# Layer 3 attention probabilities turned in 32x32 blocks on VectorE and moved through DRAM, with new orders for layers 2 and 3

## The reference

```
# layer 2 (RWKV block): token shift, five mixes, k, r, v, g, decay w; state scan; group norm; gate; Wo;
#                       layer norm; channel mix with Wfk, Wfr, Wfv
# layer 3
q = hidden_state @ Wq + bq          # 32 query heads of 16
k = encoder_hidden_state @ Wk + bk  # 8 key heads
v = encoder_hidden_state @ Wv + bv
scores = einsum('bkgld,bksd->bkgls', q, k) * scale + mask
attn = softmax(scores, axis=-1)                    # 32 heads x 128 queries x 128 keys
out = einsum('bkgls,bksd->bkgld', attn, v) @ Wo + bo
x = out + hidden_state;  return layer_norm(x) * gamma + beta
```

## Time and profile before

| what | us |
|---|---|
| median of 3 runs | 2327.11 (2327.05 to 2329.89) |
| the profiled execution, device time | 2325.5 |
| its span, first to last instruction | 2323.7 |
| of it steps 3 to 16 of layers 2 and 3 (stages p, w and a all there) | 954.83 |
| step 17 | 48.69 |
| step 18 and the last b | 45.54 |

### The profile page before, as it was taken

The page is one execution under the profiler, slowest core; times in us unless marked ns, Lnnn a source line. Parts: engine busy times, 40 slices in busy tenths (PEclk is TensorE's granted clock), DMA queues, the critical chain, the costliest instruction groups (busy, mean ns, idle before and its releaser), DMA issues.

```text
span 2323.7 us, 56522 instructions
## 1 busy us (share of the span) xinstructions
PE 2164.6 (93%) x22208; PEld 1578.5 (68%) x22208; DVE 1132.4 (49%) x3132; ACT 1164.6 (50%) x3500; POOL 567.2 (24%) x573
## 2 busy tenths in 40 slices
PE   7886799999999999998579999999999999999986
PEld 3444576666667766665367787777777877778754
DVE  4664333333333333333334566555666665566643
ACT  4553344444444444443123665655566565566554
POOL 0001000000001000000143444433344444344420
PEclk9998899999999999999779999999999999999998
DMA  5531333333333333334501001011110101110000
GB/s 167 169 112 62 103 100 102 94 95 105 101 99 103 95 91 91 91 83 119 163 16 22 18 21 27 16 26 22 27 22 21 27 16 27 22 22 20 21 19 10
DMA packets 188378, 149.06 MB, mean 64 GB/s; under 512 B 85280, under 2 KB 163488, under 8 KB 185888
## 3 DMA queue, kind: packets, MB, share of 16 engines
q1 hardware_dynamic: 177920, 115.49, 19.5%
q10 hardware_dynamic: 8032, 18.35, 2.2%
q0 software_dynamic: 2240, 12.58, 1.6%
HBM read 96.04 MB, written 46.14 MB: 61 GB/s over the span
## 4 chain that ended last, share of the span: by engine, by line
PE 47%; ACT 1%; DVE 1%; issue 1%; POOL 0%; POOLq 0%; DVEq 0%; ACTq 0%
PE bank L1561 13%; PE bank L1567 12%; PE bank L1554 4%; PE quad L1689 4%; PE quad L1694 2%; PE quad L1808 1%; PE bank L1824 1%; PE quad L1685 1%; PE bank L1590 1%; PE quad L1610 1%; PE bank L1712 1%; PE quad L1699 1%; PE bank L1724 1%; PE bank L1629 1%; PE bank L1637 1%
## 5 line engine op out<-in xcount | busy, mean ns | idle before, releaser
L782 PE MATMUL bank<-normedT,mlp_w 128*128 128x128 f32 x2048 | 242.5, 278 | 18.7 <-ACT geluT L878 17.9
L782 PEld LDWEIGHTS bank<-normedT,mlp_w 128*128 128x128 f32 x2048 | 233.7, 193 | 31.7 <-ACT geluT L878 20.7
L792 PE MATMUL bank<-mlp_w,geluT 128*128 128x512 f32 x512 | 224.7, 592 | 0.0
L2005 ACT ACTIVATE scores<-scores,nmax 128x128 f32<-128x128 f32 x512 | 198.3, 396 | 2.5 <-DVE nmax L2267 2.5
L1493 POOL TENSOR_TENSOR k_even_odd<-k_even_odd,decay_products 128x512 f32<-128x512 f32 x80 | 98.1, 1226 | 327.3 <-PE quad L1689 251.8
L792 PEld LDWEIGHTS bank<-mlp_w,geluT 128*128 128x128 f32 x512 | 95.0, 190 | 108.1 <-issue 108.1
L958 DVE CUSTOM_DVE_ANT_0 probs<-quad,neg_mask 128x256 f32<-128x256 f32 x256 | 90.8, 420 | 110.1 <-PE quad L737 110.1
L886 ACT ACTIVATE probs<-probs,nmax 128x256 f32<-128x256 f32 x256 | 126.6, 496 | 12.2 <-DVE nmax L958 11.7
L1421 POOL TENSOR_TENSOR gn_rstd<-gn_var_eps,halfs 128x32 f32<-128x32 f32 x16 | 87.0, 5435 | 170.3 <-DVE gn_var_eps L2190 170.3
L2267 DVE CUSTOM_DVE_ANT_0 scores<-quad,mask 128x128 f32<-128x128 f32 x512 | 110.9, 286 | 31.7 <-PE quad L1808 31.7
L2155 DVE TENSOR_TENSOR rT<-rT,decay_products 128x256 f32<-128x256 f32 x96 | 40.9, 426 | 175.0 <-PE quad L1689 72.0
(11 more groups left out here) (241 smaller groups left out, 4502.4 us busy)
## 6 DMA issues: line engine op xcount, KB each, us to landing
l_blocks<-probs_turned_blocks SPq DMA_DIRECT2D x128, 256.0 KB, 2.7
probsT<-l_blocks SPq DMA_DIRECT2D x256, 128.0 KB, 3.6
x_in<-in_x SPq DMA_DIRECT2D x32, 256.0 KB, 2.9
mlp_w<-in_mlp_w POOLq DMA_DIRECT2D x8, 1024.0 KB, 5.6
ctx_in<-in_ctx SPq DMA_DIRECT2D x16, 256.0 KB, 2.9
l_out<-wy ACTq DMA_DIRECT2D x16, 256.0 KB, 2.2
wy_in<-l_out SPq DMA_DIRECT2D x16, 256.0 KB, 3.8
hT<-in_ctxT SPq DMA_DIRECT2D x16, 256.0 KB, 3.5
```

What stands on the lines that cost most here:

```text
L782: mm = nc.tensor.matmul(ps[:, f * P:(f + 1) * P], mlp_w1[:, c, m * P:(m + 1) * P], nT[:, c, :], start=(c == 0), stop=(c == NC - 1))
L792: mm = nc.tensor.matmul(PS[M.bank][:, :], gT[:, f, :], mlp_w2[:, f, :], start=(f == 0), stop=(f == NF - 1))
L2005: ac = nc.scalar.activation(s, s, ACT.Exp, bias=nmax[:, k, 2 * c + e:2 * c + e + 1], scale=-1.0, accum_out=rsum[:, kv, gr:gr + 1])
```

## The change

What it does:

- `a_turn` leaves TensorE and ScalarE. The 32 transposes and 8 copies out of PSUM a batch are gone.
- The scores lie in one tile `sc` of nine slots of 512 columns. Score group k is spread over slots: `prob(k, c, e)` is four pieces of 32 columns, one in each of the four slots of its half. `a_max` and `a_exp` write and read these pieces.
- `a_turn` k on VectorE is one 128 x 512 `transpose` (16 columns of 32x32 blocks): it reads slot k+1 and writes slot k. It waits until the four exponentials of its half are done and until the turn before it is.
- `a_put` p on SyncE stores two turned slots, 512 KB, to the DRAM tensor `a_blocks`; four a batch. `a_get` half loads them with the keys on the partitions, four DMAs of 256 KB each; the first half goes to a tile `probsT`, the second back into slots 0 to 3.
- `a_value` waits for the loads. `a_norm`'s copy of the sums on GpSimd waits for the eighth turn, the copy into `attn` on ScalarE for the last store, and VectorE applies them in two pieces.
- The tile `v2` goes; its values take the place of `z`, and `n_shift` waits until they are spread.
- `ORDER` and `USES` are new on every engine.

```diff
-        sc = [sb(f"scores{u}", [P, 2, 2, P]) for u in range(NU)]
-        scT = [sb(f"probsT3_{q}", [P, 2, 2, P]) for q in range(RG)]
+        sc = sb("scores3_turned", [P, 2 * RG + 1, D])
+        scT = (sb("probsT3", [P, RG, D]), sc[:, 0:RG, :])
+        blocks3 = nc.dram_tensor("a_blocks", (2, P, RG, D), F32, kind="Internal").ap()
...
-                ("p_level", 4): ("quad", 1), ("p_level", 5): ("quad", 1), ("p_level", 6): ("quad", 1), ("p_s0",): (7, 1),
+                ("p_level", 4): ("quad", 1), ("p_level", 5): ("quad", 1), ("p_level", 6): ("quad", 1), ("p_s0",): (6, 1),
...
+        def prob(k, c, e):
+            at = 256 * e + 64 * (k % RG) + SB * c
+            return sc[:, RG * (k // RG) + 1:RG * (k // RG) + 1 + RG, at:at + SB]
...
+                def a_put(i, uses, p):
+                    half, m = p // 2, 2 * (p % 2)
+                    if later(i):
+                        sp.wait_ge(s_got[half], 16 * RG * i)
+                        sp.sem_inc(s_hold, 1)
+                    sp.wait_ge(s_turned, NU * i + 2 * p + 2)
+                    sp.dma_start(blocks3[half][:, m:m + 2, :], sc[:, 2 * p:2 * p + 2, :]).then_inc(s_put[p], 16)
+
+                def a_get(i, uses, half):
+                    if half == 0 and later(i):
+                        sp.wait_ge(s_av, 2 * i - 1)
+                        sp.sem_inc(s_hold, 1)
+                    for p in (2 * half, 2 * half + 1):
+                        sp.wait_ge(s_put[p], 16 * i + 16)
+                        sp.sem_inc(s_hold, 1)
+                    for m in range(RG):
+                        sp.dma_start(scT[half][SB * m:SB * m + SB, :, :], blocks3[half][:, m, :].rearrange("(q j) n -> j q n", q=RG))\
+                            .then_inc(s_got[half], 16)
...
-                def a_turn(i, uses, k):
-                    pe.wait_ge(s_exp, NU * i + rank("act", "a_exp", k) + 1)
-                    turn4(uses[("a_turn", k)], BANK["a_turn", k], sc[k][:, :, :, :].rearrange("p a e q -> p (a e) q"))
...
-                    for t in latest([uses[("a_turn", RG * half + r)] for r in range(RG)]):
-                        pe.wait_ge(t.free, t.done)
+                    pe.wait_ge(s_got[half], 16 * RG * (i + 1))
...
-                def a_turn(i, uses, k):
-                    u = uses[("a_turn", k)]
-                    act.wait_ge(u.ready, u.made)
-                    if k >= RG:
-                        act.wait_ge(s_av, 2 * i + 1)
-                    nc.scalar.activation(scT[k % RG][:, :, :, :].rearrange("p a e q -> p (a e) q"),
-                                         chunked(PS[BANK["a_turn", k]][:, :]), ACT.Copy).then_inc(u.free, 1)
...
+                    act.wait_ge(s_put[3], 16 * i + 16)
...
+                def a_turn(i, uses, k):
+                    half = k // RG
+                    dve.wait_ge(s_exp, NU * i + 1 + max(rank("act", "a_exp", q) for q in range(RG * half, RG * half + RG)))
+                    if k == 0 and later(i):
+                        dve.wait_ge(s_attnT, i)
+                    elif k:
+                        dve.wait_ge(s_turned, NU * i + k)
+                    dve.sem_inc(s_hold, 1)
+                    nc.vector.transpose(sc[:, k, :], sc[:, k + 1, :]).then_inc(s_turned, 1)
```

More of the change, by code:

```diff
@@ L1261, in layers23 @@
         S = {k: (sem(f"l23_{k}_psum_ready"), sem(f"l23_{k}_psum_free")) for k in ("quad", 5, 6, 7)}
-        USES = {("n_xa",): (7, 1), ("p_t5",): (6, 1), ("p_t5t",): (6, 1), ("p_mix",): ("quad", RG), ("p_mix4",): ("quad", 1),
+        USES = {("n_xa",): (6, 1), ("p_t5",): (7, 1), ("p_t5t",): (6, 1), ("p_mix",): ("quad", RG), ("p_mix4",): ("quad", 1),
                 ("p_u1",): (6, 1), ("p_w",): (6, 1), ("p_k",): (7, 1), ("p_r",): (5, 1), ("p_v",): (7, 1), ("p_g",): (6, 1),
                 ("p_level", 0): ("quad", 1), ("p_level", 1): ("quad", 1), ("p_level", 2): ("quad", 1), ("p_level", 3): ("quad", 1),
-                ("p_level", 4): ("quad", 1), ("p_level", 5): ("quad", 1), ("p_level", 6): ("quad", 1), ("p_s0",): (7, 1),
[L1268 to L1272, removed]
@@ L1273, in layers23 @@
+                ("p_level", 4): ("quad", 1), ("p_level", 5): ("quad", 1), ("p_level", 6): ("quad", 1), ("p_s0",): (6, 1),
+                ("w_var",): (7, 1), ("w_rstd",): (5, 1), ("w_out",): (5, 1), ("w_xc",): (5, 1), ("w_fk",): (5, 1), ("w_fr",): (6,
+                1), ("w_fv",): (5, 1), ("a_x",): (6, 1), ("a_q",): (6, 1), ("a_kv",): (5, 1), ("a_score", 0): ("quad", RG),
+                ("a_score", 1): ("quad", RG), ("a_norm",): (7, 1), ("b_out",): (7, 1)}
         BANK = {(k[0] if len(k) == 1 else k): bank for k, (bank, _) in USES.items()}
@@ L1275, in layers23 @@
         ORDER = dict(
-            pe=[("p_t5",), ("a_x",), ("w_var",), ("p_t5t",), ("b_out",), ("p_mix",), ("a_q",), ("a_kv",), ("p_mix4",), ("p_k",),
-                ("w_rstd",), ("a_score", 0), ("p_u1",), ("p_r",), ("a_score", 1), ("p_w",), ("w_out",), ("a_turn", 0), ("p_level",
-                0), ("p_g",), ("a_turn", 2), ("p_level", 1), ("w_xc",), ("p_v",), ("a_turn", 3), ("p_level", 2), ("a_turn", 1),
-                ("n_xa",), ("w_fr",), ("p_level", 3), ("w_fk",), ("p_level", 4), ("a_turn", 4), ("a_value", 0), ("a_turn", 7),
-                ("a_turn", 5), ("p_level", 5), ("a_turn", 6), ("w_fv",), ("p_level", 6), ("a_norm",), ("a_value", 1), ("p_s0",),
-                ("p_av",), ("p_av6",)],
@@ L1293, in layers23 @@
[L1293 to L1296 removed]
+            pe=[("p_t5",), ("a_kv",), ("p_t5t",), ("w_var",), ("p_mix",), ("a_x",), ("b_out",), ("a_q",), ("p_mix4",), ("p_k",),
+                ("w_rstd",), ("a_score", 0), ("p_u1",), ("p_r",), ("a_score", 1), ("p_w",), ("w_out",), ("p_level", 0), ("p_v",),
+                ("p_level", 1), ("w_xc",), ("p_g",), ("p_level", 2), ("w_fk",), ("p_level", 3), ("w_fv",), ("p_level", 4),
+                ("w_fr",), ("p_level", 5), ("a_norm",), ("n_xa",), ("a_value", 0), ("p_level", 6), ("a_value", 1), ("p_s0",),
+                ("p_av",), ("p_av6",)],
```

88 lines of the change are left out of this document (49 added, 39 removed).

## The result

The changed kernel takes 2370.64 us (median of 4 runs, 2356.54 to 2379.61); the kernel before took 2327.08 us beside it. The ratio is 1.018, 95% interval 1.013 to 1.023: slower, where 2278 us and a range up to 2302 us were forecast. The profiled execution took 2372.1 us.

The account below looks back on a forecast made before the run. TensorE's sum of instructions was taken to bound steps 3 to 16: 2325.5 - 58.8 (transposes) + 7 (waits) + 6 (step 18) - 3 (step 17) = 2276.7 us, with the median 1.6 above, so 2278 us; range 2264 to 2302.

Parts of the forecast that it names:

- Steps 3 to 16 are TensorE's sum, and 4.2 us of transposes leave each: TensorE, 14 steps: time is its sum of instructions; removing transposes takes 68.20 us steps to 64.0, 58.8 us in all.
- The cover for the trip: Last turn to second `a_value`: TensorE's other work leaves 13.4 us to hide the store and load through DRAM.
- VectorE's turns are hidden: VectorE, each step: eight turns of 0.67 us add 5.4 us, giving 46.9 of 64.0 us, not near the bound.
- 0.5 us of small waits a step: Steps 3 to 16: slips where little time is spare cost 0.5 us a step (bounds 0 and 1.5), 7 us back.
- four tight places: Level 5 to 6, second `a_score`, `p_mix` and `w_fv`: 0 to 0.4 us to spare each; not all will hold.
- two norm products: VectorE, stage b, ahead of the second `a_score`'s maxima: 1.66 us each beside busy GpSimd, 0.75 with it idle.
- the first rival: Many small waits: TensorE waits 2.5 us a step on VectorE's turns and products at new places; 2306 us, chance 0.17.
- The trip costs nothing in steps 3 to 16: Store and load through DRAM: 9.5 us, upper bound 10.8, so 3.9 us of cover is left over, at worst 2.6.
- the second rival: The trip through DRAM is late, 17.4 us, and the second `a_value` holds TensorE each step; 2350 us, chance 0.05.
- Steps 17 and 18, 3 us longer together: Tail of the kernel: step 18 with the trip on its path 6 us slower, step 17 3 us faster.
- the shortening of step 17: Step 17: 4.2 us of transposes go and `w_fk` comes ahead of `w_fr`; 3 us faster, bounds 6 faster, 2 slower.

Follow-up runs that it names:

- thin loads: The changed kernel with each of its eight loads a step cut to 32 of 512 columns, 128 KB instead of 2 MB a step; 2275.43 us, ratio 0.978.
- loads by row block: The changed kernel with each load writing one slot on all 128 partitions instead of four slots on 32, same bytes and 2 KB pieces; 2520.79 us, ratio 1.083.
- first half early: The changed kernel with the first half's loads ahead of the last two stores in SyncE's queue, and x's load ahead of the second half's; 2393.09 us, ratio 1.029.
- loads apart: The changed kernel with the second half's four loads issued only after the first half's four have landed; 2385.64 us, ratio 1.026.
- foreign copies: The kernel before with 2 MB of stores a step and four unawaited 1 MB DRAM-to-DRAM copies issued at once; 2371.53 us, ratio 1.018.
- half of the columns: The changed kernel with each load cut to 256 of 512 columns, 1 MB a step instead of 2; 2281.99 us, ratio 0.981.
- copies of 5.1 us in the kernel before: The kernel before with 2 MB of stores and eight unawaited 256 KB DRAM-to-DRAM copies a step added; 2328.96 us, ratio 1.001.
- copies of 4.6 us behind thin loads: The changed kernel with loads of 32 of 512 columns and four unawaited 256 KB DRAM-to-DRAM copies behind each half's loads; 2303.73 us, ratio 0.989.
- wide loads: The changed kernel with one 1 MB load a half, 8 KB pieces on 128 partitions, and each store split in four; 2298.41 us, ratio 0.990.

## Why the prediction was wrong

Its sum was 2276.7 us, the profiled execution 2372.1: 95.4 us off. Of these, 977.76 - 903.0 = 74.8 us are in steps 3 to 16 (903.0 is 954.83 - 58.8 + 7), 115.9 - 97.2 = 18.7 us in steps 17 and 18 (53.36 + 62.56 against 48.69 + 45.54 - 3 + 6), and 2.0 us ahead of step 3. Step by step:

- *Steps 3 to 16 are TensorE's sum, and 4.2 us of transposes leave each:* right. With thin loads a step is 64.33 us; 64.0 was the sum. The cover for the trip was right too: 13.4 us, and 13.4 to 13.7 measured.
- *VectorE's turns are hidden:* right. A turn takes 0.706 us (0.67 was taken), VectorE has 46.1 us a step (46.9), and TensorE does not wait for it in steady steps.
- *0.5 us of small waits a step:* too much. With thin loads TensorE idles for 0.2 us a step, and none of the four tight places showed. Of the two norm products, the one that took 1.66 us takes 0.74 in its new place, the other still 1.55. The forecast and the first rival both leaned on a danger that was not there.
- *The trip costs nothing in steps 3 to 16:* here it failed, in two ways. First the size. 9.5 us were taken from the last turn to the landing, 10.8 as the upper bound; it is 16.0, beyond the cover. 4.5 us to landing were taken for a load, and 5.7 and 8.5 us were measured. Layer 1's loads are half as large and no other megabyte is in the queue with them; 10.8 us is the sum of its slowest single store and load, and not, as the second rival has it, the time of a half. Then, and above all, the question that was asked. I asked when the data would be there, and never what 2 MB in flight do to something else on the same engines. 35.3 us of stalls on "issue", and 34.8 us at a lower clock behind all stalls, are in no term and in no rival. Of the 46.0 us of idle TensorE only 8.3 are waits for these loads; without the stalls they would be some 32, by the estimate above.
- *Steps 17 and 18, 3 us longer together:* they are 21.7 us longer. From the first scores of step 18 to the last values are 2352.42 - 2319.88 = 32.5 us, 27.6 were forecast. With thin loads step 17 takes 49.6 us and step 18 takes 52.7, where 45.7 and 51.5 were forecast: the shortening of step 17 did not come. TensorE waits 4.3 us there for `gn_dev` and 3.5 us for `ffn_k_in`, stage w's chain through VectorE; before, 1.7 us for `gn_dev` were the longest of these. The other 13.6 us come with real loads: TensorE waits 13.8 us for them (2.2 with thin loads), and the clock of step 18 is 0.64 (0.71).
- *The second rival* gave 2350 us from a late trip, at 0.05. It had the sign and half of the mechanism. It said that the change loses from a trip of about 16 us on, and the trip is 16.0 us; but it gave all of the loss to awaited data, in each step. They were awaited in 5 of 14, and the 12 stalls on "issue" are not in it. In the slower experiments (loads by row block, first half early, loads apart) its mechanism does appear, with 3 us and more in each step.

What is shown: the loss in steps 3 to 16 comes with the bytes of the loads, not with the orders or turns. TensorE stalls on instruction packets that start late under a deep backlog; foreign copies do the same to the kernel before and cost it 45 us, with no data awaited. Loads that move faster give most of the loss back. A second half that lands 18 us after the turns is awaited for 3 us in every step. What is not shown is how the changed kernel's 77.8 us would split if only one of the two, late fetches or late data, were taken away. The Trainium skill describes the instruction stream as blocks of 16 KiB through a DMA queue of its own, its cost "mostly hidden" (Runtime: NRT & Kernel Launch, Instruction fetch mechanics); the trace agrees with the size of the packets and, under a backlog, not with the cost: up to 4.25 us. It also says that a DMA engine takes turns between queues packet by packet (DMA: Bandwidth & Descriptors, Queues, rings and completion order). No row shows what a fetch waits for before its packet starts, so whether such turns can delay it by 1.9 to 5.1 us stays open.

Open too is from what backlog on it begins; landing times do not decide it. On "issue", in 14 steps: 0.2 us with half of the columns (landing after 3.4 and 3.8 us), 0.9 us with copies of 5.1 us in the kernel before, but 13 us with copies of 4.6 us behind thin loads; 12 and 14 us with loads of 5.2 to 5.7 us (loads apart, first half early), 35 us with 5.7 and 8.5 us (the changed kernel), 30 us with copies of 10.2 us, but 2.5 us with wide loads of 6.3 and 8.1 us. The place in the step counts as well, since a fetch comes only every 9 us. Why loads of 256 KB into 32 partitions move at 215 GB/s where wide ones move at some 350 and more was not taken apart: partitions per DMA and bytes per piece changed together.

## What to carry to other kernels

Cost a new transfer twice: when it lands, and what it does to everything else that uses the DMA engines while it is in flight, the instruction streams of the engines included. Where the profile shows a bound engine idle on "issue" in the middle of a group of short instructions, look at the DMA share and at the packets of the instruction queue in that stretch, and at the granted clock behind it. Count a trip from the last turn to the last landing, with all loads of the burst in it, before calling it hidden: a stall elsewhere can cover a landing that is late. Before giving up such a change, change the form of the transfer: here long pieces over all partitions in few DMAs turned 2% slower into 1% faster.

## What was not expected of the hardware

- A backlog of DMA traffic in which TensorE has no part, copies that land after 10.2 us, stalls TensorE for up to 4.8 us at a time (2371.53 us for the kernel before with copies, against 2326.25 us).
- After a stall TensorE goes on 2.2 to 3.1 us after a 16 KB packet of its instruction queue starts, in all 45 stalls on "issue" of 0.8 us and more in steps 3 to 16 of five runs. In the changed kernel the packet takes as long as ever (median 1.05 us) and starts 1.9 to 5.1 us late.
- A stall costs almost twice: 43.0 us of idle time came with 34.8 us of work at a lower clock. In the step shown the clock went to 0.50 in the stall and was back at 1.00 some 4 us after TensorE resumed.
- 256 KB loads from DRAM into 32 partitions, 2 KB a piece, hold all DMA engines at a share of 1.05 for 215 GB/s; 1 MB loads over 128 partitions with 8 KB pieces reach 373 GB/s at 1.01; loads with an outermost dimension of 4 use a share of 0.30 at 111 GB/s.
